# Key row product and next batch's statistics interleaved with V's residuals on VectorE; its small scalar operations in tensor-tensor form

## What is computed

```python
x = x + attn(layernorm(x), queries, combiners)
x = x + xattn(layernorm(x), ctx, ctx, Wq, bq, Wk, bk, Wv, bv)
x = x + ffn(layernorm(x), router_w, router_b, w_gate, w_up, w_down, sw_gate, sw_up, sw_down)

def xattn(query, key, value, ...):
    q, k, v = query @ Wq + bq, key @ Wk + bk, value @ Wv + bv
    return softmax(q @ k.T / sqrt(512)) @ v
```

## Time and profile before

| what | value |
|---|---|
| median of 3 runs | 2009.5 us (2008.22 to 2009.92) |
| the profiled execution, its time | 2010.12 us |
| its span in the profile | 2008.4 us |
| PE busy | 1921.1 us (96%) |
| DVE, ACT, POOL busy | 42%, 33%, 40% |
| chain that ended last | PE 66% (line 70: 43%, line 1252: 21%) |

### The profile page before, as it was taken

One profiled execution on the slowest core, in us unless ns is written; L12 is line 12 of the kernel. 1 busy time (PEld: TensorE's weight loads), 2 busy tenths in 40 slices (PEclk: granted clock), 3 DMA queues, 4 the chain that ended last, 5 costly groups with the idle time before them and its releaser, 6 DMA issues.

```text
span 2008.4 us, 27705 instructions
## 1 busy us (share of the span) xinstructions
PE 1921.1 (96%) x10672; PEld 1695.8 (84%) x10672; DVE 837.5 (42%) x1896; ACT 670.5 (33%) x1366; POOL 809.5 (40%) x662
## 2 busy tenths in 40 slices
PE   8989889889898999999999999999999999999997
PEld 5778778678786778888889999999999999999996
DVE  2575584685674332222233333333333333333332
ACT  3344443434443311111133333333333233333321
POOL 2132241241344330000255566665565665565631
PEclk9999989899898999999999999999999999999999
DMA  7021311312315533223354454554444554444521
GB/s 269 1 91 36 126 69 58 126 44 83 106 53 180 185 67 70 68 63 95 65 129 102 108 130 118 122 129 101 111 128 119 121 127 102 113 127 117 125 38 26
DMA packets 106738, 203.40 MB, mean 101 GB/s; under 512 B 14800, under 2 KB 14800, under 8 KB 106352
## 3 DMA queue, kind: packets, MB, share of 16 engines
q1 hardware_dynamic: 81312, 148.52, 23.5%
q0 software_dynamic: 25296, 53.11, 15.0%
HBM read 135.92 MB, written 65.68 MB: 100 GB/s over the span
## 4 chain that ended last, share of the span: by engine, by line
PE 66%; DVE 1%; ACT 1%; issue 0%; POOL 0%; ACTq 0%; DVEq 0%; POOLq 0%
PE ps L70 43%; PE ps L1252 21%; PE ps L1194 2%; ACT buffer L1070 0%; DVE buffer L1143 0%; DVE buffer L1158 0%; ACT L1108 0%; DVE stats L483 0%; ACT buffer L1108 0%; ACT buffer L349 0%; PE ps L663 0%; PE ps L669 0%; POOL out_tokens L1059 0%; ACT lg L409 0%; DVE buffer L1183 0%
## 5 line engine op out<-in xcount | busy, mean ns | idle before, releaser
L70 PE MATMUL ps<-buffer,buffer 128*128 128x320 f32 (+1 forms) x6816 | 1242.2, 344 | 57.7 <-DVE buffer L546 51.1
L70 PEld LDWEIGHTS ps<-buffer,buffer 128*128 128x128 f32 x6816 | 1118.9, 190 | 169.3 <-issue 55.9
L1014 POOL TENSOR_TENSOR buffer<-buffer,buffer 128x512 fp32r<-128x512 f32 x289 | 387.7, 1506 | 232.6 <-ACT buffer L1070 232.3
L1252 PE MATMUL ps<-buffer,buffer 128*128 128x512 f32 x1904 | 457.1, 394 | 3.6 <-DVE buffer L1143 3.6
L1252 PEld LDWEIGHTS ps<-buffer,buffer 128*128 128x128 f32 x1904 | 351.0, 188 | 76.6 <-POOL buffer L1014 3.2
L1158 DVE TENSOR_TENSOR buffer<-ps,buffer 128x320 f32<-128x320 f32 (+1 forms) x240 | 127.5, 532 | 605.3 <-ACT buffer L1108 562.5
L1108 ACT ACTIVATE buffer<-ps 128x320 f32<-128x320 f32 (+1 forms) x240 | 112.4, 469 | 653.4 <-PE ps L70 639.7
L1070 ACT ACTIVATE buffer<-buffer 128x512 fp32r<-128x512 f32 (+3 forms) x529 | 269.6, 563 | 55.6 <-PE ps L1252 50.5
L1059 POOL DMA_INDIRECT out_tokens<-buffer,slot_index x80 | 125.6, 1570 | 220.0 <-DVE buffer L1183 207.3
L1143 DVE TENSOR_TENSOR buffer<-buffer,buffer 128x320 fp32r<-128x320 f32 (+1 forms) x240 | 183.4, 764 | 12.0 <-ACT buffer L1070 10.8
L316 POOL TENSOR_TENSOR buffer<-buffer,buffer 128x512 fp32r<-128x512 f32 x32 | 41.0, 1312 | 350.1 <-ACT buffer L344 350.1
(11 more groups left out here) (109 smaller groups left out, 970.3 us busy)
## 6 DMA issues: line engine op xcount, KB each, us to landing
buffer<-in_wts SPq DMA_DIRECT2D x289, 256.0 KB
tokens_normed_T<-buffer SPq DMA_DIRECT2D x16, 1024.0 KB, 5.5
buffer<-tokens_normed_T SPq DMA_DIRECT2D x16, 1024.0 KB, 6.5
buffer<-in_x SPq DMA_DIRECT2D x8, 1024.0 KB, 5.2
buffer<-in_ctxT SPq DMA_DIRECT2D x8, 1024.0 KB, 9.5
tokens_normed<-buffer SPq DMA_DIRECT2D x8, 1024.0 KB, 4.8
out_tokens<-buffer SPq DMA_DIRECT2D x8, 1024.0 KB, 4.3
out_tokens<-buffer POOLq DMA_DIRECT2D x32, 256.0 KB, 3.8
```

The source lines that it names most:

```text
L70: last = pe.matmul(out, left, right, start=(i == 0), stop=(i == len(todo) - 1))
L1014: pool.tensor_tensor(wl[n % RING][:], wraw[n % RAW][:], wh[n % RING][:].bitcast(F32), ALU.subtract).then_inc(s_wl, 1)
L1252: ins = pe.matmul(down_bank[n % 2][:], left, right, start=(c == 0 and i == 0), stop=(c == FC - 1 and i == len(passes) - 1))
```

## The change

It does four things. `KROW` is no step any more: its products go into VectorE's part of `V`. There each of the four tiles now has a product with `key_row`, the `bn_stats` of the next batch's tile, and V's residual, in turn; the bias is added behind the last. `ST0` stands behind `V` and only aggregates (in pass -1, for batch 0, it still does all). `Y2T` stands ahead of `LN0` on every engine. And three small operations (the sum with eps, the bit operation, and the bias on `krow`) get a second tensor operand in place of a scalar one: a column `eps_col` or `qbias` broadcast, and a tile `flip` of -1.

```diff
-    magic = sb("magic", [P, NT], I32)
+    magic, flip = sb("magic", [P, NT], I32), sb("flip", [P, NT], I32)
+    eps_col = sb("eps_col", [P, 1], F32)
...
+        pool.memset(flip[:], -1)
+        pool.memset(eps_col[:], EPS)
...
-            link(dve.tensor_scalar(veps[:], mv[:, :, 1], EPS, None, ALU.add))
-            link(dve.tensor_scalar(rstd[k][:].bitcast(I32), veps[:].bitcast(I32), 1, -1,
-                                   ALU.logical_shift_right, ALU.bitwise_xor))
+            link(dve.tensor_tensor(veps[:], mv[:, :, 1], eps_col[:].to_broadcast([P, NT]), ALU.add))
+            link(dve.scalar_tensor_tensor(rstd[k][:].bitcast(I32), veps[:].bitcast(I32), 1, flip[:],
+                                          ALU.logical_shift_right, ALU.bitwise_xor))
...
             if name == "ST0":
-                dve.wait_ge(s_x[b % XS], 16 * (b // XS + 1))
-                deviations(0, b, s_y0)
+                if b == 0:
+                    dve.wait_ge(s_x[0], 16)
+                deviations(0, b, s_y0, counted=b >= 1)
...
             if name == "V":
-                for t in range(NT):
+                dve.wait_ge(s_y1, NT * (b + 1))
+                if b >= 1:
+                    filled(dve, "PT", b - 1, NT - 1)
+                for t in range(NT):
+                    last = dve.tensor_tensor_reduce(krow_products[:, t, :], y[:, t, :], key_row[:], 1.0, 0.0,
+                                                    ALU.mult, ALU.add, krow[:, t:t + 1])
+                    if b + 1 < B:
+                        if t == 0:
+                            dve.wait_ge(s_x[(b + 1) % XS], 16 * ((b + 1) // XS + 1))
+                        last = statistics(b + 1, t)
+                    if t == NT - 1:
+                        link(last)
                     dve.wait_ge(s_vh, NT * b + t + 1)
                     bank = bank_of("V", b, t)
                     dve.tensor_tensor(vl[:, t, :], bank[:], vh[:, t, :].bitcast(F32), ALU.subtract)\
                         .then_inc(s_ev["V"], 1)
...
-                dve.tensor_scalar(krow[:], krow[:], qbias[:, 2 * NC:2 * NC + 1], None, ALU.add)\
+                dve.tensor_tensor(krow[:], krow[:], qbias[:, 2 * NC:2 * NC + 1].to_broadcast([P, NT]), ALU.add)\
                     .then_inc(s_krow, 1)
...
-        steps = [("Y1T", i), ("KROW", i), ("ST0", i + 1), ("V", i), ("LN0", i + 1), ("Y2T", i - 1), ("INIT", i + 1),
+        steps = [("Y1T", i), ("V", i), ("ST0", i + 1), ("Y2T", i - 1), ("LN0", i + 1), ("INIT", i + 1),
```

More of the change, by code:

```diff
@@ L477, in inverse_deviation, with statistics, deviations @@
                 link(dve.scalar_tensor_tensor(rstd[k][:], rt[:], 1.5, rstd[k][:], ALU.add, ALU.mult))
-        def deviations(k, b, used):
-            src = x[b % XS]
-            for t in range(NT):
-                last = dve.bn_stats(stats[:, t, :], src[:, t, :])
-            link(last)
+        def statistics(b, t):
+            return dve.bn_stats(stats[:, t, :], x[b % XS][:, t, :])
+        def deviations(k, b, used, counted=False):
+            if not counted:
+                for t in range(NT):
+                    last = statistics(b, t)
+                link(last)
             for t in range(NT):
@@ L542, in step @@
             if name == "V":
[L543 to L548, removed]
                 dve.wait_ge(s_y1, NT * (b + 1))
@@ L555, in step @@
                                                     ALU.mult, ALU.add, krow[:, t:t + 1])
-                link(last)
-                dve.tensor_scalar(krow[:], krow[:], qbias[:, 2 * NC:2 * NC + 1], None, ALU.add)\
+                    if b + 1 < B:
[3 more added lines that the diff above has]
+                    if t == NT - 1:
+                        link(last)
+                    dve.wait_ge(s_vh, NT * b + t + 1)
+                    bank = bank_of("V", b, t)
+                    dve.tensor_tensor(vl[:, t, :], bank[:], vh[:, t, :].bitcast(F32), ALU.subtract)\
+                        .then_inc(s_ev["V"], 1)
+                dve.tensor_tensor(krow[:], krow[:], qbias[:, 2 * NC:2 * NC + 1].to_broadcast([P, NT]), ALU.add)\
                     .then_inc(s_krow, 1)
```

## The result

The changed kernel takes 1958.67 us (median of 4 runs, 1954.47 to 1958.97) against 2009.71 before (4 runs, 2008.22 to 2010.51): a ratio of 0.9742, 95% interval 0.9725 to 0.9759. The prediction was 1948.2. The gain came as foreseen and is 2.6% instead of 3.0%; some 10 us are missing. The profiled execution took 1958.95 us with a span of 1957.2, where the sum said 1947.1.

A forecast was written before the change was run, and what follows sets the result against it. TensorE was taken to bound the kernel, stalling before Q for VectorE's residuals of V. Span 2008.4 - 51.1 - 15.7 + 5.5 = 1947.1, adjusted to a forecast time of 1948.2 us; range 1942 to 1966, chance 0.89.

The forecast's parts named there:

- V's residuals move up: Ahead of Q: with V's residuals earlier on VectorE, all seven TensorE stalls go whole, -51.1 us.
- The clock: In the seven Qs: without the stall TensorE keeps its upper clock, 2.25 us back from each, -15.7 us in all.
- Rival 4: In Q: the stalls go but the clock still dips after the light transposes, 1964 us; chance 0.08.
- Batch 0: Before the first Q: products and statistics ahead of Y1T's residuals start Q 4.8 us later and lengthen it, +5.5 us.
- A product waits for at most one addition, not for the run: VectorE's key products meeting GpSimd's additions: the two take turns, each product held 1.24 us at most.
- rival 2: V's step on VectorE: products held for GpSimd's whole run, LP waits half a microsecond, 1951 to 1957 us; chance 0.06.
- I put all this at 0, hidden under Q: Work behind V's last residual, through Y2T's residuals, LN0, copies and writes: later but covered, with 2.1 us slack before LP.
- the first sign that the prediction named for being wrong: In TensorE's list of waits: a wait for Y2T's residual ahead of LP would show the forecast wrong.
- belong to batch i-1 and are read in phase 2: SyncE's writes of Y2T's output, y2l among them: their changed timing was taken to cost nothing, 0 us.
- The small operations: The eps sums, bit operations and krow sums in two-tensor form: cost 0, bounds -1 to +2 us overall.
- rival 3: The small chain before Y2T's residuals meets GpSimd's additions, making LP late seven times, 1970 to 1986 us; chance 0.07.
- Rival 5: Slower: VectorE's chain between V's last residual and Y2T's residuals is held each pass, LP takes over the stall; chance 0.02.

The follow-up runs named there:

- e5: The changed kernel with batch 0's products and statistics back behind Y1T's residuals, as before the change: 1950.47 us (ratio 0.9711 to the kernel before).
- e7: The changed kernel with each of GpSimd's four additions of y2 to x waiting for the one before: 1966.86 us (0.9793 of the kernel before).
- e3: The changed kernel with GpSimd's additions of y2 to x cut to 16 of 512 columns: 1946.52 us (0.9693 of the kernel before).
- e6: The changed kernel with y2l in rows of its own, so ScalarE need not wait for its write: 1954.22 us (0.9735 of the kernel before).
- e1: The changed kernel with its three small operations back in scalar form, new order kept: 1955.97 us (0.9743 of the kernel before).
- e2: The kernel before with only the three small operations put in tensor-tensor form: 2008.15 us (1.0002 of the kernel before).
- e12: The changed kernel with Y2T behind LN0 again on every engine: 1986.52 us (0.9889 of the kernel before).
- e4: The changed kernel with all four products and the krow sum ahead of V's residuals: 1978.87 us (0.9853 of the kernel before).
- e8: The changed kernel with GpSimd's additions of y2 ahead of its indirect DMAs of pair lists: 1977.26 us (0.9844 of the kernel before).

## Why the prediction was right, and where it missed

**V's residuals move up: right.** The term of -51.1 came to -50.8 in this execution (0.3 us stay, in pass 7, where the hold is 8.47).

**The clock: right.** The Qs of passes 1 to 6 run in 11.14 to 11.17 us, where the term took 11.15, and that of pass 7 in two pieces of 5.73 and 5.74. Rival 4 is out. The seven together gave back 15.4 us instead of 15.7.

**Batch 0: right in kind, half a microsecond short.** Idle time 7.81 - 2.06 = 5.75 and Q 13.05 - 12.74 = 0.31 make +6.1, against +5.5. The turns with GpSimd cost more than the 0.4 allowed: the first product took 1.01 and the second 1.80. The part in Q is one execution's: against e5's Q of 11.17 it would be 1.88.

**"A product waits for at most one addition, not for the run": wrong.** This is the step that failed. It was read off pass 1, where the products meet additions that themselves wait tile by tile for ScalarE's `y2` and so have gaps. In passes 2 to 6 the additions follow each other, and the product is held 5.3 us for the run; e7 shows that a wait between the additions brings the 1.6 back, and e3 that there is no hold with additions of 16 columns. For the products, rival 2 is what happened, and its chance of 0.06 was too small: the row that was nearest to the case was not that of the same instruction in another pass but that of another instruction against the same run, the 5.23 of the earlier trace rows. The Trainium skill, "SBUF — State Buffer", section "SBUF: two separate sides", names VectorE instructions "with two SBUF inputs" among those that lock the pair of ports against GpSimd. By that rule, the trace agrees: product and tensor-form sum are both held. It says that the pair is taken for the whole instruction; here the hold runs over four instructions (5.32), and over six in pass 7 (8.47).

**"I put all this at 0, hidden under Q": wrong by 7.6 us.** Two waits came out. LP waits for Y2T's residual, 4.1 us in five: the first sign that the prediction named for being wrong, and rival 2's mechanism. Half a microsecond was said, 0.68 to 1.14 measured; the difference is in good part the start of the additions, which the prediction left where it was and which the longer last indirect DMA moves by 0.3 to 0.5 us. And T waits for ScalarE, 3.5 us in four, which the prediction excluded with the sentence that the writes "belong to batch i-1 and are read in phase 2". That is true of the data and not of the memory: ScalarE waits for the same write before it refills `y2l`'s rows. e6 shows it. In the kernel before, a pass was 8 to 9 us longer (77.9 to 78.4 from Q to Q behind pass 2, now 69.2 to 70.0, where 67 to 68 was foretold) and the list has no such wait.

**The small operations: right at 0.** e1 and e2 show that the form neither earns nor costs what can be measured.

**The range.** The time, 1958.67, lies above the forecast's own 1943 to 1954 and above rival 2's 1951 to 1957, whose 3 us more at batch 0 didn't come and which knew nothing of T's wait. It is inside 1942 to 1966 because the range was drawn up to rival 4, and rival 4 did not happen. That part is luck.

**The sum, again.** 1947.1, and 4.1 for LP, 3.5 for T, 0.6 for batch 0, 0.3 for pass 7, and 0.9 - 0.4 for phase 2's wait (line 1263, 4.5 now and 3.6 before) and the first weights (7.8, before 8.2) make 1956.1 of the 1957.2 measured. The last 1.1 us are busy time, as far as the rows show: 0.3 is what the Qs gave back less, and LP (2.11 to 2.13 instead of 2.00, five times) and T (3.67 instead of 3.60, four times) run 0.9 longer behind their waits.

**Slower, and the other rivals.** The small chain didn't meet the additions (rival 3): the product had already been held to the end of the run, and the chain ran behind it, `shift` ready at 286.2. Rival 5's mechanism, LP taking over the stall, is real but small here; e12 shows it grown, at 24.2 us, by another cause than the one named. Its LP waits for ScalarE's copies behind LN0.

## What to carry to other kernels

An instruction of VectorE that is cheap by itself can cost the length of what GpSimd does beside it. Before moving one, see against which run it would stand, and whether the other engine waits between its instructions there: the same pair in another pass, where it does, is no guide for one where it doesn't. And ask of every write to memory not only who reads the data, but who waits to overwrite the buffer it leaves from; when a pass gets shorter, that wait is the next one.

## What was not expected of the hardware

- A VectorE instruction that meets GpSimd's additions of 512 columns is held until the end of the run when they follow back to back (5.2 to 5.3 us beside runs of 4.96 to 5.03), and takes 1.6 to 1.8 us in all when something separates them, even only a wait for the addition before (e7). Additions of 16 columns back to back don't hold it (0.72, e3). It makes no difference whether it is a product over 512 columns, a sum of two tensors over 4, or a sum with a scalar column over 4. What decides it inside the chip, the gap itself or which engine comes first at each one, stays open.
- The hold can begin before the run: in e4, in e2 and in the kernel before, the sum starts 0.2 us ahead of the first addition, beside an indirect DMA of GpSimd, and is held all the same. The other way round, a product that starts beside an indirect DMA can make that one longer: 1.50 us instead of 0.98 in pass 3 of the kernel after.
- In e8 the write of `y2l`, 1 MB, took 13.3 us from its issue to its landing with eight indirect DMAs ahead of it and beside it, 8.4 in the kernel after and 8.2 in e3; the medians of the 16 writes of Y2T are 5.5 us before and 8.1 after.
